# Decay differences of a state-space mixer: rows loaded by DMA, bound added in PSUM, exponential read from PSUM

## The reference, cut to what matters

```
A_dt  = (dt * A)                                   # [chunk token, head]
A_cum = cumsum(A_dt)                               # within a chunk
L     = exp(segsum(A_dt))                          # exp(A_cum[l] - A_cum[s]) for s <= l, else 0
Y_diag[l,h,:] = sum_s (C_l . B_s) * L[h,l,s] * x[s,h,:] * dt[s,h]
states        = sum_s B_s * exp(A_cum[-1] - A_cum[s]) * x[s,h,:] * dt[s,h]
Y_off[l,h,:]  = (C_l . previous state) * exp(A_cum[l])
y = (Y_diag + Y_off + D * x) * silu(gate);  y is normalized by group;  out = y @ out_proj.T
```

## Time and profile before

| | |
|---|---|
| median of three runs | 3512.9 us (3508.41 to 3513.11) |
| span of the profiled execution | 3506.6 us |
| mean granted TensorE clock | 0.954 of full speed |
| TensorE busy | 3137.1 us, 89% of the span |
| VectorE busy | 2278.1 us, 65% |
| ScalarE busy | 1005.0 us, 29% |
| GpSimd busy | 660.5 us, 19% |
| DMA, mean | 31 GB/s |

### The profile page before, as it was taken

How to read it: one execution, slowest core, us unless ns; L and a number is a source line. 1 busy time by engine, 2 the same in 40 slices (tenths; PEclk the granted TensorE clock), 3 DMA queues, 4 the chain that set the end, 5 groups by cost and what they waited for, 6 DMA issues and landing times. The chain is left out here.

```text
span 3506.6 us, 40196 instructions
## 1 busy us (share of the span) xinstructions
PE 3137.1 (89%) x11856; PEld 1686.1 (48%) x11856; DVE 2278.1 (65%) x3726; ACT 1005.0 (29%) x2369; POOL 660.5 (19%) x441
## 2 busy tenths in 40 slices
PE   2899899988989989899898998988799799999989
PEld 1444454444544445444454454544684433333368
DVE  4777777777777777776777767665546455555354
ACT  1322323223232232232222322322213233333321
POOL 1122122122222212212222221222210000000021
PEclk7899999999999999999999999998899899999999
DMA  5000010010010001001001100000104100000000
GB/s 169 13 22 4 25 49 13 1 65 19 4 59 25 4 25 50 13 1 65 19 4 56 28 4 19 33 0 1 64 0 166 50 28 22 27 22 27 9 7 18
DMA packets 48126, 107.68 MB, mean 31 GB/s; under 512 B 9104, under 2 KB 18400, under 8 KB 45248
## 3 DMA queue, kind: packets, MB, share of 16 engines
q1 hardware_dynamic: 42624, 102.47, 8.8%
q10 hardware_dynamic: 5312, 2.92, 0.3%
HBM read 86.23 MB, written 19.14 MB: 30 GB/s over the span
## 5 line engine op out<-in xcount | busy, mean ns | idle before, releaser
L439 PE MATMUL bank<-xnT,wh 128*128 128x512 f32 x1280 | 592.4, 607 | 124.4 <-DVE sg L842 92.2
L528 PE MATMUL bank<-wg,xnT 128*128 128x512 f32 x1024 | 482.3, 615 | 0.0
L580 PE MATMUL bank<-wo,ggT 128*128 128x512 f32 x1024 | 466.0, 609 | 0.5 <-ACT ggT L689 0.5
L439 PEld LDWEIGHTS bank<-xnT,wh 128*128 128x128 f32 x1280 | 241.2, 194 | 410.8 <-issue 278.1
L733 DVE SCALAR_TENSOR_TENSOR cacc<-raw,cwh,cacc 128x512 f32<-128x512 f32 x480 | 390.3, 813 | 17.0
L580 PEld LDWEIGHTS bank<-wo,ggT 128*128 128x128 f32 x1024 | 201.7, 198 | 237.7 <-issue 232.3
L1821 PE MATMUL bank<-at_PT,at_vz 128*49 128x512 f32 (+3 forms) x768 | 298.5, 499 | 0.8 <-ACT at_yTs L1890 0.8
L528 PEld LDWEIGHTS bank<-wg,xnT 128*128 128x128 f32 x1024 | 193.4, 199 | 197.3 <-issue 197.3
L1914 DVE TENSOR_REDUCE at_nm<-bank 128x1 f32<-128x512 f32 (+3 forms) x256 | 151.1, 591 | 206.4 <-PE bank L1783 161.8
L503 PEld LDWEIGHTS bank<-xch,em 128*128 128x128 f32 x2048 | 237.4, 194 | 55.2 <-issue 52.2
L503 PE MATMUL bank<-xch,em 128*128 128x64 f32 x2048 | 243.5, 278 | 6.4 <-DVE em L791 2.4
(11 more groups left out here) (243 smaller groups left out, 4655.3 us busy)
## 6 DMA issues: line engine op xcount, KB each, us to landing
wh<-w_hs_dram SPq DMA_DIRECT2D x80, 256.0 KB, 2.7
wg<-w_gate_dram SPq DMA_DIRECT2D x8, 2048.0 KB, 7.7
wo<-w_out_dram SPq DMA_DIRECT2D x8, 2048.0 KB, 8.7
qk_scratch<-at_part SPq DMA_DIRECT2D x48, 256.0 KB
at_qT<-qk_scratch SPq DMA_DIRECT2D x32, 192.0 KB, 2.6
at_kT<-qk_scratch SPq DMA_DIRECT2D x32, 192.0 KB, 2.6
pk<-pack_scratch SPq DMA_DIRECT2D x16, 272.0 KB, 3.1
wgu<-w_gu_dram SPq DMA_DIRECT2D x1, 3584.0 KB, 11.3
```

The lines of the kernel that those rows point to most:

```text
L439: mm = nc.tensor.matmul(BA[bank][:, :], wh[:, j, k, :], xnT[:, k, h * HALF:(h + 1) * HALF], start=(k == 0), stop=(k == KC - 1))
L528: mm = nc.tensor.matmul(BA[b][:, :], xnT[:, k, ttok], wg[:, k, u * 512:(u + 1) * 512], start=(k == 0), stop=(k == KC - 1))
L580: mm = nc.tensor.matmul(BA[b][:, :], ggT[:, j, :], wo[:, j, :], start=(j == 0), stop=(j == JT - 1))
```

## The change

The three parts of `A_cum` go to DRAM as rows per head (tokens along the row), with both signs, in a scratch tensor `rows_dram` of their own, and are no longer in `pack` (80 instead of 136 numbers per token and group). In the first block TensorE makes the cumulated sums once more with heads on the partitions (eight 128 x 128 matmuls), and VectorE cuts them there. For each step SP loads two pieces of three rows into `RW` (one buffer for all steps): rows 0 to 2 of the moving side hold the positive parts of the 16 heads and rows 3 to 5 of the stationary side the negative ones, the others hold ones, and rows 6 to 127 zeros. TensorE adds the causal bound (-1e30 above the diagonal, `negq`) with an identity matmul of 512 columns and then one 128-column matmul per head. ScalarE takes the exponential straight from the bank, and the bank is free when ScalarE has read it. Instead of five instructions `dv_small` is one copy of 256 columns.

```diff
 def pe_pre(pe, g, z):
-            pe.wait_ge(d_pk[h], 32 * g + 32)
-            dv_sm.wait(pe, 5 * n)
+            dv_sm.wait(pe, n)
             nc.tensor.matmul(sm[:, 0:P], ...)
-            nc.tensor.transpose(sm[:, P:2 * P], act2[:, h, JB, tok], ident[:, :])
-            nc.tensor.transpose(sm[0:PK, 2 * P:2 * P + P // 2].bitcast(BF16),
-                                pk[:, h, c, O_PARTS:PACK].bitcast(BF16), identb[:, :]).then_inc(pe_sm.sem, 1)
+            nc.tensor.transpose(sm[:, P:2 * P], act2[:, h, JB, tok], ident[:, :]).then_inc(pe_sm.sem, 1)
 def pe_diff(pe, g, z, quarters):
-            dv_sm.wait(pe, 5 * n + 5)
+            if quarters[0] == 0:
+                pe.wait_ge(d_rw, 32 * n + 32)
             for q in quarters:
-                dv_mn.wait(pe, 4 * n + q - 1)
-                nc.tensor.matmul(BD[q % 2][:, :], Lp[:, :], Rp[:, q * 512:(q + 1) * 512],
-                                 start=True, stop=True).then_inc(pe_df.sem, 1)
+                ac_ex.wait(pe, 4 * n + q - 1)
+                nc.tensor.matmul(BD[q % 2][:, :], identb[:, :], negq[:, :], start=True, stop=False)
+                for i in range(QH):
+                    hh = slice((q * QH + i) * P, (q * QH + i + 1) * P)
+                    mm = nc.tensor.matmul(BD[q % 2][:, i * P:(i + 1) * P], RW[:, 0, hh], RW[:, 1, hh],
+                                          start=False, stop=(i == QH - 1))
+                mm.then_inc(pe_df.sem, 1)
 def ac_exps(act, g, z, quarters):
+            pe_yd.wait(act, 2 * n)
             for q in quarters:
-                dv_mn.wait(act, 4 * n + q + 1)
-                nc.scalar.activation(em[:, q, :], em[:, q, :], ACT.Exp).then_inc(ac_ex.sem, 1)
+                pe_df.wait(act, 4 * n + q + 1)
+                nc.scalar.activation(em[:, q, :], BD[q % 2][:, :], ACT.Exp).then_inc(ac_ex.sem, 1)
 def dv_small(dve, g, z):
-            (copies of pS, Lp and Bs, product CBm, product Rp)
+            nc.vector.tensor_copy(BC[:, z % 2, :], sm[:, 0:2 * P]).then_inc(dv_sm.sem, 1)
-def dv_min(...)                      and its calls in dv_slot and in the prologue
 def dv_masked: CBm -> BC[:, z % 2, 0:P]
 def po_pre: + pool.wait_ge(d_pk[h], 32 * g + 32)
 SP:
+                for i in range(QH):
+                    sp.dma_start(negq[:, i * P:(i + 1) * P], A["negm"][:, 1, :]).then_inc(s_cst, 16)
+                def load_rows(g, z):
+                    for side, at in ((1, 0), (0, 1)):
+                        sp.dma_start(RW[PARTS * side:PARTS * side + PARTS, at, :].rearrange("i (h l) -> i h l", h=HG),
+                                     rows_dram[side, :, bass.ds(g * HG, HG), z * P:(z + 1) * P]).then_inc(d_rw, 16)
+                def next_rows(g, z):
+                    pe_df.wait(sp, 4 * (8 * g + z + 1))
+                    sp.sem_inc(turned, 1)
+                    load_rows of the step after (g, z)
                 with sp.Fori(0, G - 1) as g:
+                    for z in range(4):
+                        next_rows(g, z)
                     po_cw.wait(sp, 2 * g + 1)
                     load_taps(g + 1, 0)
                     for i in range(PT):
+                        if i in (4, 7):
+                            next_rows(g, 4 if i == 4 else 5)
                         pe_P.wait(sp, (2 * g + 1) * PT + i + 1)
                         load_tile(sp, g + 1, i)
                     ...
                     load_pack(g + 1, 0)
+                    next_rows(g, 6)
+                    next_rows(g, 7)
                     pe_gt.wait(sp, 2 * (8 * g + 8))
                     load_gate(sp, g + 1)
                     pe_out.wait(sp, 8 * g + 8)
                     load_out(sp, g + 1)
                     load_pack(g + 1, 1)
 POOL prologue: memsets of RW (128 rows, then 6) in place of those of Lp and Rp
 first block: + 8 matmuls (rem[:, z], mask) on TensorE, cuts of the sums into `part` on VectorE,
              + one DMA rows_dram <- part (1.5 MB); pack is 80 instead of 136 numbers wide
```

More of the change, by code:

```diff
@@ L178, in mixer @@
             pack = sb(c0, "pack", [P, NT, G, PACK])
+            part = sb(c0, "part", [P, 2, PARTS, T], BF16)
             XCUT = ((0, 2), (2, NT // 2), (NT // 2, NT))
@@ L271, in _ @@
                         mm = nc.tensor.matmul(BANK[4 + i][:, :], mask[:, :], rem[:, i * 512:(i + 1) * 512],
+                                              start=True, stop=True)
+                    for z in range(NT):
+                        mm = nc.tensor.matmul(BANK[z // CH][:, (z % CH) * P:(z % CH + 1) * P], rem[:, z * P:(z + 1) * P], mask[:, :],
                                               start=True, stop=True)
@@ L343, in _ @@
                     chain(o)
-                    dve.wait_ge(p_cst, 2)
+                    for i in range(2):
+                        o = nc.vector.tensor_copy(v2[:, i * 512:(i + 1) * 512], BANK[i][:, :])
+                    chain(o)
+                    src = v2
+                    for i in range(PARTS):
+                        chain(nc.vector.tensor_copy(part[:, 0, i, :], src[:, :]))
+                        if i < PARTS - 1:
+                            chain(nc.vector.tensor_tensor(rem[:, :], src[:, :], part[:, 0, i, :], ALU.subtract))
+                            src = rem
+                    chain(nc.vector.tensor_scalar(part[:, 1, :, :], part[:, 0, :, :], -1.0, None, ALU.mult))
+                    dve.wait_ge(p_cst, 1)
                     z4 = lambda ap: ap.rearrange("p (z g h) -> p z g h", z=NT, g=G)
-                    pb = pack[:, :, :, O_PARTS:PACK].bitcast(BF16)
                     chain(nc.vector.tensor_copy(pack[:, :, :, O_DT:O_DT + HG], z4(dt[:, :])))
@@ L466, in pe_hidden @@
             if u == 1:
-                dv_sm.wait(pe, 5 * n + 4)
+                dv_sm.wait(pe, n + 1)
             for i in range(4):
@@ L519, in state @@
                     dv_yd.wait(pe, 2 * n + u + 1)
-                    nc.tensor.matmul(BY[u][:, :], Bs[:, z % 2, :], xd[:, u * 512:(u + 1) * 512],
+                    nc.tensor.matmul(BY[u][:, :], BC[:, z % 2, P:], xd[:, u * 512:(u + 1) * 512],
                                      start=True, stop=True).then_inc(pe_st.sem, 1)
@@ L775, in dv_xdt @@
                 .then_inc(dv_xc.sem, 1)
[L777 to L783, removed]
         def dv_masked(dve, g, z):
             n = 8 * g + z
-            dv_sm.wait(dve, 5 * n + 4)
+            dv_sm.wait(dve, n + 1)
             for q in range(NQ):
@@ L869, in dv_slot @@
             silu(0)
-            if not last:
-                dv_min(dve, *nxt, (2, 3))
             conv(2)
@@ L990, in _ @@
                     load_pack(g + 1, 1)
+                for z in range(NT - 1):
+                    next_rows(G - 1, z)
             @block.gpsimd
@@ L1020, in prologue @@
                 def prologue(bank):
-                    act.wait_ge(s_set, 5)
+                    act.wait_ge(s_set, 4)
                     for i in range(PT):
```

83 lines of the change are left out of this document (32 added, 51 removed).

## The result

The changed kernel takes 3567.93 us (median of four runs, 3565.2 to 3569.3) against 3512.55 us before: a ratio of 1.016 with a 95% interval of 1.0145 to 1.0174. Between the medians lie 55.4 us. The span of its profiled execution is 3566.7 us, 60.1 us more than before, with a mean granted clock of 0.948.

The account below looks back on a forecast made before the run. TensorE (89% busy) was taken to bound the kernel, apart from three kinds of wait. Terms +36 - 31 - 8 + 65 - 2 = +60 us gave 3573 us (3512.9 + 60), range 3525 to 3610 us.

Parts of the forecast that it names:

- TensorE's added work: Per-head 128-column matmuls at 0.055 us each add 0.8 us per step, on the path in 45 long slots: +36 us.
- VectorE's relief: Slots z = 1, 2, 5, 6: of 3.1 us taken out, 1.0 reaches TensorE's wait for `sg`, 30 times: -31 us.
- The clock behind these waits: Behind the 30 waits for `sg`, a wait a third shorter gives back part of 12.6 us: -8 us.
- The new wait in short slots: 18 short slots: TensorE's quarter 2 waits for ScalarE's late exponential; projection +2.7 us later, 0.9 us slower: +65 us.
- First block and first step: Extra fp32 matmuls and VectorE work, changed DMA traffic, a vanished stall and larger memsets: together -2 us, within 5.
- the stall of 2.36 us before the first `Y_diag`: First step: TensorE's stall of 2.36 us before L503 was to go.
- the memsets of `RW`: First block: larger memsets may cost 1 us.
- The step from span to median: Runs' median taken to lie 6.3 us above the span, so 3566.6 us of span became 3573 us.
- Rival 2: TensorE's small matmuls are bound by weight loads, 0.115 us each: +52 us, 3625 us; chance 0.08.
- rival 3: Rows land 10 us late, TensorE waits 4 us in slot 0 of seven passes: 3605 us; chance 0.04.
- rival 4: Short slots lose nothing, since TensorE was waiting there anyway: +9 us, 3522 us; chance 0.06.
- Rival 1: At the 30 waits for `sg`, VectorE's relief reaches TensorE in full: -6 us, 3507 us; chance 0.10.

Follow-up runs that it names:

- b3: Kernel before with each 512-column matmul of the differences made as four of 128 columns with the same weights: 3536.52 us, ratio 1.0085.
- a6: Changed kernel without row loads (SP's waits kept) and without the four identity matmuls per step: 3539.09 us, ratio 1.0077 to the kernel before.
- a2: Changed kernel with GpSimd's addition waiting until VectorE has finished the left-over convolution: 3505.4 us, ratio 0.9983 to the kernel before.
- a1: Changed kernel with ScalarE's exponentials 0 and 1 of short slots taken before its wait for the gated output: 3508.19 us, ratio 0.9991.
- b1: Kernel before with only the bank's release changed: TensorE's differences wait for the exponential instead of the minimum: 3601.9 us, ratio 1.0253.
- b2: Kernel before with GpSimd's addition moved after the left-over convolution: 3478.81 us, ratio 0.9911.
- b8: Kernel before with GpSimd's addition after left-over convolution and activation, and hd after product yt in short slots: 3411.27 us, ratio 0.9718.
- a3: Changed kernel with exponentials 0 and 1 early in short slots and GpSimd's addition after the left-over convolution: 3451.63 us, ratio 0.9829.
- a7: Changed kernel with early exponentials, later GpSimd addition, and in short slots GpSimd's hd after VectorE's product yt: 3392.35 us, ratio 0.9664.
- a8: Changed kernel with early exponentials, hd after yt, and GpSimd's addition after left-over convolution and, in short slots, activation: 3360.71 us, ratio 0.9576.
- a5: Changed kernel without any load of rows, SP's waits kept, so the differences are a constant: 3565.96 us, ratio 1.0156 to the kernel before.

## Why the prediction was right

*TensorE's added work*: forecast +0.8 us per long slot, measured 0.94 in slots z = 0 and 4. The rate per matmul was right (b3, a6); the 0.14 us over it also appears in b3, where four matmuls with the same weights stand in place of one.

*VectorE's relief*: forecast 1.0 of 3.1 us per slot, measured 1.19 (3.08 to 1.89). The forecast let L737 take its full 0.54 us behind the end of GpSimd's addition; it ended 0.28 us behind it, which is about the difference. That running beside the addition takes the rest is shown by a2, where the addition alone was moved and 1.4 us more of the wait went. The Trainium skill has the rule that VectorE and GpSimd share a port pair, which the first instruction that needs it holds to its end ("SBUF — State Buffer", the section on who interferes with whom). The trace agrees: 2.46 us for L737 beside L916, 0.54 alone.

*The clock behind these waits*: forecast -8 us, measured -1.7: six of seven tiles still take 5.40 us, behind 1.89 us of wait. This step failed. I took a shorter wait to mean less lost clock. The number of slow tiles does not follow the wait: behind 1.89 us there are six (after), four (a1) and 13 (a6), behind 3.08 us seven (before), 16 (b3) and 23 (b1). Behind 2.15 us there are eight (b2) and 11 (b8), and only behind 0.5 us there is none (a2, a3, a7, a8).

*The new wait in short slots*: forecast 18 x 3.6 = 65 us, measured 54.3, 3.0 each. The delay of the projection was right (+2.67 against +2.7 us); the projection itself lost 0.4 instead of 0.9 us. a1 and b1 show that it is this wait.

*First block and first step*: forecast -2, measured +2.5 us in these two executions. This difference is no property of the change: the first slot ends at 185.94 us in the traced execution of the changed kernel, but at 183.3 to 184.4 in those of a1, a2, a3, a5, a6 and a7 and at 185.62 in a8, which all have its first block, and at 183.4 to 186.7 in those of the kernel before, b1, b2, b3 and b8. One part of the forecast failed in all the changed ones: the stall of 2.36 us before the first `Y_diag` did not go. TensorE waits twice for `em` there, 0.91 and 1.20 us in the changed kernel. Another was forecast as 1 us: the memsets of `RW`. Six partitions take as long as 128, so ScalarE starts its first copy only when GpSimd is done, at 92.34:

```profile
85.20 3.51 POOL L1008 MEMSET RW<- 128x4096 bf16 x1
...
88.77 3.50 POOL L1010 MEMSET RW<- 6x4096 bf16 x1
...
92.34 0.19 ACT L720 COPY raw<-zero 128x3 f32<-128x3 f32 x1 [28.96 <-POOL half L1011]
```

That is 6.07 us behind the start of TensorE's first tile (86.27). In the kernel before the copy waits for that tile and starts 5.67 us behind it (83.98 to 89.65), so the memsets cost about 0.4 us.

The sum came out at 60.1 us of span against 60 forecast, and that closeness is luck. The misses have both signs: about +6 us in TensorE's added work, -5 in VectorE's relief, +6 in the clock, -11 in the short slots and +4 up to the end of the first slot. And between the medians the change is 55.4 us, 3567.93 where 3573 was forecast. The step from span to median was read wrongly: in every run here the span lies about 2 us under the time of its own execution (3566.7 and 3568.49 us for the changed kernel), so most of the 6.3 us is that the traced execution of the kernel before was a fast one. Rival 2 is refuted by b3 and the timelines, rival 3 by a5, rival 4 by a1 and b1. Rival 1 did not happen as made, and a2 shows its condition: with the addition out of the way the relief reaches TensorE.

What stays open is the rule by which TensorE's clock falls. Equal waits are followed by tiles of 3.70, 5.40 or 6.63 us, and runs that differ in a little other work (0.14 us per slot in b3) have other numbers of slow tiles; that the shift of this work is the cause is not shown, and no run here shows a quantity that tells beforehand.

## What to carry to other kernels

When a buffer's release moves to another engine, look up where in that engine's fixed order the releasing instruction stands in every kind of slot: here it was early in 45 slots and behind `ggT` in 18, and moving one block of two lines was worth 60 us. Work taken off VectorE only helps if what runs next does not then collide with GpSimd; move GpSimd's start behind the operations on the path. Price a stall on TensorE by more than its length, and give the price a wide range: here it could be named only after the run.

## What was not expected

Lost clock was as large as the waits. In b1 38.5 us of added wait cost 90 us; in a7 28 us less wait gave 59 us back. Splitting matmuls, which added 0.14 us per slot, cost 24 us, most of it in slower tiles elsewhere. A GpSimd memset of 4096 bf16 elements takes 3.50 us on 6 partitions and 3.51 us on 128.
